# Regrouping the second expert layer of a two-layer transformer kernel: steps of 3, 4, 3 and 2 groups

## The reference

```
x: 2048 tokens of 128;  16 experts, hidden width 256, top 2
mag    = x @ bank_mag[e]
freq   = x @ bank_freq[e]
hidden = tanh(mag) * cos(softplus(freq) + 0.1 + bank_phase[e])
out    = hidden @ bank_down[e]
y      = sum over the two chosen experts of weight * out
y      = y * rsqrt(mean(y * y) + 1e-6) * norm_w
result = x + gate * y
```

## Time and profile before

| what | us |
|---|---|
| median of three runs | 714.82 (712.31 to 719.94) |
| profiled execution, whole | 713.9 |
| its span | 712.1 |
| PE busy | 493.4 |
| DVE busy | 468.7 |
| ACT busy | 336.3 |
| POOL busy | 410.8 |
| mean granted TensorE clock, share of full | 0.814 |

### The profile page before, as it was taken

How to read it: one execution, slowest core, us unless ns; L and a number is a source line. 1 busy time by engine, 2 the same in 40 slices (tenths; PEclk the granted TensorE clock), 3 DMA queues, 4 the chain that set the end, 5 groups by cost and what they waited for, 6 DMA issues and landing times.

```text
span 712.1 us, 8241 instructions
## 1 busy us (share of the span) xinstructions
PE 493.4 (69%) x2183; PEld 318.4 (45%) x2183; DVE 468.7 (66%) x911; ACT 336.3 (47%) x652; POOL 410.8 (58%) x321
## 2 busy tenths in 40 slices
PE   3577979998998899735777796269530588687410
PEld 2233323433433333524776786126530487587410
DVE  6958898898999899771332233648535566576717
ACT  3265863674675464111222235374310089589605
POOL 0039899999898989216666654612575102545650
PEclk9877989999998799856699799569555599989765
DMA  5043334442233330014656583400011555533125
GB/s 183 0 152 118 118 128 171 122 138 104 90 114 111 105 121 26 16 34 145 191 174 205 170 241 103 113 1 0 19 52 61 190 190 196 182 138 122 34 74 145
DMA packets 58384, 81.85 MB, mean 115 GB/s; under 512 B 7569, under 2 KB 32658, under 8 KB 58338
## 3 DMA queue, kind: packets, MB, share of 16 engines
q1 hardware_dynamic: 51010, 69.97, 30.2%
q0 software_dynamic: 5024, 10.30, 4.7%
q10 hardware_dynamic: 2304, 1.05, 0.5%
HBM read 57.82 MB, written 11.14 MB: 97 GB/s over the span
## 4 chain that ended last, share of the span: by engine, by line
PE 47%; DVE 15%; ACT 12%; issue 8%; another core or an unknown queue 6%; DMA 4%; POOL 4%; ACTq 2%; SPq 1%; POOLq 0%; DVEq 0%
PE ps L1128 13%; PE ps L1246 5%; PE ps L1235 4%; PE ps L1095 4%; DVE hs L1770 4%; PE ps L1404 4%; PE ps L1122 4%; PE ps L1416 2%; PE ps L1286 2%; POOL bu L568 2%; ACTq L941 1%; DVE prod L1780 1%; ACT mag L979 1%; ACT freq L981 1%
## 5 line engine op out<-in xcount | busy, mean ns | idle before, releaser
L568 POOL TENSOR_TENSOR bu<-uT,b_sb 128x1024 f32<-128x1024 f32 x64 | 150.9, 2379 | 29.0 <-DVE uT L1750 29.0
L539 POOL DMA_INDIRECT y_dram<-ys,rows_i x86 | 91.0, 1058 | 118.7 <-DVE ys L2010 70.3
L1128 PE MATMUL ps<-prod,cst 128*128 128x512 f32 x256 | 130.2, 653 | 2.9 <-DVE yT L1790 2.9
L749 ACT ACTIVATE ps<-dtT,neg_a 128x512 f32<-128x512 f32 x128 | 85.4, 684 | 50.6 <-DVE hs L1770 50.1
L1128 PEld LDWEIGHTS ps<-prod,cst 128*128 128x128 f32 x256 | 50.2, 207 | 81.5 <-issue 77.1
L579 POOL TENSOR_TENSOR prod<-hs,c_sb 128x1024 f32<-128x1024 f32 x32 | 76.6, 2394 | 15.2 <-PE ps L1128 10.8
L1770 DVE TENSOR_TENSOR_SCAN hs<-ps,carry,bu 128x512 f32<-128x512 f32 x64 | 77.6, 1262 | 4.8 <-ACT ps L749 4.5
L1770 DVE TENSOR_TENSOR_SCAN hs<-ps,bu 128x512 f32<-128x512 f32 x64 | 73.7, 1203 | 3.7 <-ACT ps L749 3.6
L1246 PE MATMUL ps<-w_s,ht 128*128 x312 | 48.5, 305 | 23.9 <-ACT ht L838 12.2
L838 ACT ACTIVATE ht<-ps,b1T 128x128 f32<-128x128 f32 x78 | 24.5, 368 | 82.4 <-PE ps L1235 45.1
L1404 PE MATMUL ps<-xt,mfr 128*128 128x128 f32 x376 | 53.1, 296 | 6.9 <-DVE freq L1973 3.2
(11 more groups left out here) (289 smaller groups left out, 856.3 us busy)
## 6 DMA issues: line engine op xcount, KB each, us to landing
b_sb<-b_rows SPq DMA_DIRECT2D x32, 512.0 KB
mfr<-mf_s SPq DMA_DIRECT2D x47, 256.0 KB
w1r<-in_w SPq DMA_DIRECT2D x39, 256.0 KB
c_sb<-b_rows SPq DMA_DIRECT2D x32, 256.0 KB
mf_s<-in_mf SPq DMA_DIRECT2D x16, 256.0 KB
xl<-x_slots SPq DMA_DIRECT2D x47, 64.0 KB
w_s<-in_w SPq DMA_DIRECT2D x9, 256.0 KB, 4.0
down_s<-in_down SPq DMA_DIRECT2D x16, 128.0 KB
```

Source lines behind the costliest of these rows:

```text
L539: pool.indirect_dma_start(y_dram[l], bass.IndirectOffsetOnAxis(ap=rows_i[:, 1, j:j + 1], axis=0), ys[:, j % slots, :], None).then_inc(save ...
L568: nc.gpsimd.tensor_tensor(bu[:, g % RING, :, :], uT[:, c % 2, :, :], b_sb[:, k % BRING, g % 2, :].unsqueeze(1).broadcast_to([P, ND, CHUNK] ...
L749: nc.scalar.activation(decay_of(g, d), dtT[:, c % 2, d, :], ACT.Exp, scale=neg_a[:, d, n:n + 1]).then_inc(S["a_ready"], 1)
L1128: last = nc.tensor.matmul(bank(Y_BANK + d), ident, prod[:, g % RING, d, :], start=n == 0, stop=n == NS - 1)
```

## The change

The steps get 3, 4, 3 and 2 groups instead of four times 3. Which groups' sines, products and down pairs a step does is given by two small functions, `trig_of` and `downs_of`. In the last step the down pairs begin one pair earlier and go two to a pair, and VectorE's third product there is made at the second pair. The last two groups, which have no step behind them, get their tanh, sine and product by pairs of tiles (`trig_pair`, `hidden_pair`) instead of by groups, and each pair's down product waits for its own pair's product alone (`hidden_done`). On VectorE the copies at the fifth and sixth pair of a step now stand ahead of the arguments there. The ring `mag` keeps its 24 tiles. The diff:

```
@@ -43,9 +43,9 @@
 GT = 4
 NG = (ST1 + GT - 1) // GT
 NPAIR = (ST1 + 1) // 2
-QG = 3
-QP = 2 * QG
-QUARTERS = NG // QG
+MAGS = 24
+STEP_GROUPS = (3, 4, 3, 2)
+LAST = 2 * (NG - STEP_GROUPS[-1])
 MR = 4
 LN_EPS = 1e-5
 RMS_EPS1 = 1e-5
@@ -278,7 +278,7 @@
         slot_i, pick_end = place("slot_i", [P, 2, NTILE], I32, at=e)
 
         mfr, e = place("mfr", [P, 2 * MR, 2 * H1], at=w_end)
-        mag, e = place("mag", [P, 2 * QG * GT, H1], at=e)
+        mag, e = place("mag", [P, MAGS, H1], at=e)
         ys1, e = place("ys1", [P, 2 * XR, C], at=e)
         inner_i, _ = place("inner_i", [P, NPACK[1]], I32, at=max(e, pick_end))
 
@@ -370,8 +370,39 @@
 
         def group_slots(g):
 
-            at = GT * g % (2 * QG * GT)
+            at = GT * g % MAGS
             return slice(at, at + group(g).stop - group(g).start)
+
+        def pair_slots(p):
+
+            at = 2 * p % MAGS
+            return slice(at, at + len(pair(p)))
+
+        def first_group(k):
+
+            return sum(STEP_GROUPS[:k])
+
+        def trig_of(k, i):
+
+            if k == 0:
+                return ()
+            first = first_group(k - 1)
+            if k == 1:
+                return (first + i,) if i < 3 else ()
+            at = ((0,), (1, 2), (3,))[i] if i < 3 else ()
+            return tuple(first + a for a in at if a < STEP_GROUPS[k - 1])
+
+        def downs_of(k, i):
+
+            if k == 0:
+                return ()
+            first, late = 2 * first_group(k - 1), 1 if k == len(STEP_GROUPS) - 1 else 2
+            at = ((0, 1), (2, 3), (4, 5) if k > 1 else (4,), (6, 7) if k > 1 else (5,))[i - late] if late <= i < late + 4 else ()
+            return tuple(first + a for a in at if a < 2 * STEP_GROUPS[k - 1])
+
+        def hidden_done(p):
+
+            return p // 2 + 1 if p < LAST else LAST // 2 + p - LAST + 1
 
         block = ctx.enter_context(nc.Block())
 
@@ -958,11 +989,11 @@
 
             def mag_copy(p):
 
-                n, at = len(pair(p)), 2 * p % (2 * QG * GT)
+                n = len(pair(p))
                 act.wait_ge(S["mag_ps1"], p + 1)
-                if p >= 2 * QP:
-                    act.wait_ge(S["dn_ps1"], p - 2 * QP + 1)
-                nc.scalar.activation(mag[:, at:at + n, :].rearrange("p a h -> p (a h)"), ps[:, 3 + p % 2 * 2, 0:n * H1],
+                if p >= MAGS // 2:
+                    act.wait_ge(S["dn_ps1"], p - MAGS // 2 + 1)
+                nc.scalar.activation(mag[:, pair_slots(p), :].rearrange("p a h -> p (a h)"), ps[:, 3 + p % 2 * 2, 0:n * H1],
                                      ACT.Copy).then_inc(S["mag_sb1"], 1)
 
             def softplus_tail(g):
@@ -980,26 +1011,35 @@
                 act.wait_ge(S["turned1"], g + 1)
                 nc.scalar.activation(freq[:, group(g), :], freq[:, group(g), :], ACT.Sin, scale=-TURN).then_inc(S["trig1"], 1)
 
+            def trig_pair(p):
+
+                js = slice(2 * p, 2 * p + len(pair(p)))
+                act.wait_ge(S["mag_sb1"], p + 1)
+                nc.scalar.activation(mag[:, pair_slots(p), :], mag[:, pair_slots(p), :], ACT.Tanh)
+                act.wait_ge(S["turned1"], p // 2 + 1)
+                nc.scalar.activation(freq[:, js, :], freq[:, js, :], ACT.Sin, scale=-TURN).then_inc(S["trig1"], 1)
+
             copy_xt1(0)
             copy_xt1(1)
-            for k in range(QUARTERS):
-                for i in range(QP):
-                    p = k * QP + i
+            for k, groups in enumerate(STEP_GROUPS):
+                g = first_group(k)
+                for i in range(2 * groups):
+                    p = 2 * g + i
                     freq_abs(p)
                     if p + 2 < NPAIR:
                         copy_xt1(p + 2)
                     mag_copy(p)
-                    if k and i < QG:
-                        trig((k - 1) * QG + i)
-                    if k and i == QG - 1:
+                    for done in trig_of(k, i):
+                        trig(done)
+                    if trig_of(k, i) and not trig_of(k, i + 1):
                         act.preload_act_table_set(LOG_EXP)
                     if i in (2, 3):
-                        softplus_tail(k * QG + i - 2)
-                    if i == QP - 1:
-                        softplus_tail(k * QG + 2)
+                        softplus_tail(g + i - 2)
+                    if i in (5, 7):
+                        softplus_tail(g + i // 2)
                 act.preload_act_table_set(SILU_TANH_SIN)
-            for g in range(NG - QG, NG):
-                trig(g)
+            for p in range(LAST, NPAIR):
+                trig_pair(p)
 
             def squares(c):
 
@@ -1407,31 +1447,28 @@
 
             def down_pair(p):
 
-                pe.wait_ge(S["hid1"], p // 2 + 1)
+                pe.wait_ge(S["hid1"], hidden_done(p))
                 if p >= 2:
                     pe.wait_ge(S["dn_sb1"], p - 1)
                 for j in pair(p):
                     e = expert1(j)
                     for k in range(FK1):
-                        last = nc.tensor.matmul(ps[:, 6 + p % 2, j % 2 * C:(j % 2 + 1) * C], mag[:, j % (2 * QG * GT), k * P:(k + 1) * P],
+                        last = nc.tensor.matmul(ps[:, 6 + p % 2, j % 2 * C:(j % 2 + 1) * C], mag[:, j % MAGS, k * P:(k + 1) * P],
                                                 down_s[:, bass.ds(e, 1), k, :].rearrange("p a c -> p (a c)"), start=k == 0, stop=k == FK1 - 1)
                 last.then_inc(S["dn_ps1"], 1)
 
             turn_pair(0)
             turn_pair(1)
             pe.wait_ge(S["in_down"], 16 * E1)
-            for k in range(QUARTERS):
-                for i in range(QP):
-                    p, d = k * QP + i, (k - 1) * QP
+            for k, groups in enumerate(STEP_GROUPS):
+                for i in range(2 * groups):
+                    p = 2 * first_group(k) + i
                     up_pair(p)
                     if p + 2 < NPAIR:
                         turn_pair(p + 2)
-                    if k and i in (2, 3):
-                        down_pair(d + 2 * i - 4)
-                        down_pair(d + 2 * i - 3)
-                    if k and i > 3:
-                        down_pair(d + i)
-            for p in range(NPAIR - QP, NPAIR):
+                    for d in downs_of(k, i):
+                        down_pair(d)
+            for p in range(LAST, NPAIR):
                 down_pair(p)
 
         @block.vector
@@ -2000,6 +2037,12 @@
                 dve.wait_ge(S["trig1"], g + 1)
                 nc.vector.tensor_tensor(m, m, freq[:, group(g), :], ALU.mult).then_inc(S["hid1"], 1)
 
+            def hidden_pair(p):
+
+                m = mag[:, pair_slots(p), :]
+                dve.wait_ge(S["trig1"], hidden_done(p))
+                nc.vector.tensor_tensor(m, m, freq[:, 2 * p:2 * p + len(pair(p)), :], ALU.mult).then_inc(S["hid1"], 1)
+
             def copy_y(p):
 
                 dve.wait_ge(S["dn_ps1"], p + 1)
@@ -2009,40 +2052,38 @@
                 n, at = len(pair(p)), 2 * p % (2 * XR)
                 nc.vector.tensor_copy(ys1[:, at:at + n, :].rearrange("p t c -> p (t c)"), ps[:, 6 + p % 2, 0:n * C]).then_inc(S["dn_sb1"], 1)
 
-            for k in range(QUARTERS):
-                for i in range(QP):
-                    p, d, g = k * QP + i, (k - 1) * QP, k * QG
-                    take_up(p)
+            for k, groups in enumerate(STEP_GROUPS):
+                g, final = first_group(k), k == len(STEP_GROUPS) - 1
+                for i in range(2 * groups):
+                    take_up(2 * g + i)
                     if i == 0 and k:
                         turns(g - 1)
+                    if k and i < 3 and i < groups:
+                        hidden(first_group(k - 1) + i)
+                    for d in downs_of(k, i):
+                        copy_y(d)
+                    if final and i == 1:
+                        hidden(first_group(k - 1) + 2)
+                    if k == 2 and i == 2:
+                        hidden(first_group(k - 1) + 3)
                     if i == 3:
-                        if k:
-                            copy_y(d + 2)
-                            copy_y(d + 3)
                         argument(g)
                         turns(g)
-                    if i == 4:
+                    if i == 4 or final and i == 3:
                         argument(g + 1)
-                        if k:
-                            copy_y(d + 4)
                     if i == 5:
                         turns(g + 1)
-                        if k:
-                            copy_y(d + 5)
                         argument(g + 2)
-                    if k and i < QG:
-                        hidden(g - QG + i)
-                    if k and i == 2:
-                        copy_y(d)
-                        copy_y(d + 1)
+                    if i == 7:
+                        turns(g + 2)
+                        argument(g + 3)
             turns(NG - 1)
-            hidden(NG - 3)
-            hidden(NG - 2)
-            copy_y(NPAIR - 6)
```

(8 more changed lines are left out.)

## The result

The changed kernel took 719.58 us in the median of 21 runs, the kernel before 714.24 in 21 runs beside it; the ratio is 1.0084 (1.0062 to 1.0107). The change made it slower by some 6 us, where 4 us of gain were forecast. The profiled execution of the changed kernel has a span of 719.9 us.

The account below looks back on a forecast made before the run. No engine is full; ScalarE paces the steady part, and the limit turns to GpSimd's scatters. Last scatter 689.66 to 685.9 is -3.8 us: 710.1 from the profiled 713.9, 711.0 from the median; forecast 710.4, range 705 to 716.

Parts of the forecast that it names:

- Step 0: First step: unchanged, nothing gained or lost; first batch of scatters still starts at about 599.50.
- the ring of 24 tiles: Buffer ring: stays 24 tiles and no product is late for it.
- step 1: Two more pairs and one more group add 4.6 us of unhidden ScalarE work.
- step 2: Four old and three new groups: 24.1 us plus 0 to 2.1 of waits, taken as 25.2.
- step 3: Two new groups behind three: 16.8 us; final load at 664.1, or 669.0 if 4.9 us of old waits return.
- 35 scatters: GpSimd's run from 634.8: 51.1 us, so the last scatter ends at 685.9 instead of 689.66.
- The hold of a scatter by a two-input VectorE instruction: GpSimd: a scatter starting inside such an instruction is held until it ends; floor 1.26 us each, second batch 1.56.
- GpSimd is never again out of work: From the second batch on: old waits of 5.88 and 4.17 us go; the wait before that batch grows by 4.6.
- ScalarE's chain ended last, and not the scatters: Rival on the kernel's end: scatters faster, 6 to 9 us gained, 704.6 to 707.7 us; chance 0.22.
- the tail: Last two groups by pairs: first copy ends 5.7 us after the final load, 7.3 in the old kernel.
- my sum with waits: Final load at 669.0 if old waits return, so the first of the last 7 tiles goes out at 675.0.
- The slow one: Rival: step 2 bound by TensorE from its third pair, up to 33.1 us, kernel 715.6 us; chance 0.10.

Follow-up runs that it names:

- chip 2: Quiet chip: the changed kernel run again beside the kernel before, 671.0 us against 671.9, ratio 0.998.
- chips 1 and 2: Two quiet chips: the changed kernel repeated against the kernel before, 671.2 us against 672.0 (0.996) and 671.0 against 671.9 (0.998).
- chip 12: Chip with the kernel before at 718.4 us: changed kernel 720.3, without second-layer scatters 697.4, with direct GpSimd transfers instead 701.1.
- after_fourth: The changed kernel run unaltered a fourth time, on chip 12, against the kernel before: 720.3 us against 718.4, ratio 1.006.

## Why the prediction was wrong

**Where it held.** Step 0 and the ring of 24 tiles went as counted, and step 1 nearly: it grew by 3.4 us in the first comparison and by 5.3 on chip 2, where I had 4.6. On chips 1 and 2 the whole schedule held: GpSimd never out of work after the second batch began, 25.4 us for step 2 (I took 25.2), 18.5 and 17.3 for step 3 (16.8), and on chip 2 35 scatters in 48.4 us (51.1 forecast, a mean of 1.39 each with the gap instead of 1.47). Yet the gain there is 0.2 and 0.4% by the ratios, because the old steps lacked their waits on these chips too. The hold of a scatter by a two-input VectorE instruction is seen again: the one of 646.18 ended at 647.85, 0.83 after VectorE's of 645.79 with 1.23.

**The step that failed** is step 2's "between 0 and 2.1 us of waits". It came to 30.7 us, 6.6 beyond its work of 24.1, and to 28.2 on chip 12. I had seen that step 1 waited 9 us and step 3 4.9 beyond its work, named the places and carried them over as if they belonged to the places: step 1's waits were kept, step 3's too in the later of my two values, and step 2's were taken from the old step 2. They go with the trains of scatters. In the old schedule two of the three trains beside running steps showed them, 11.2 us over the steps of chip 2 (81.7 against 70.4). In the new one all three did: 87.7 against 72.3, 15.4 us, and 85.1 on chip 12, 12.8. Without the indexed scatters they are gone on chip 12; the chip of the first comparison was not tried so. From that follows the rest. "GpSimd is never again out of work" failed on these chips alone, with idle times of 1.98, 4.62, 1.96 and 2.21; ScalarE's chain ended last, and not the scatters: the first copy of the tail was done at 687.65, against 669.0 + 5.7 = 674.7 in my sum with waits, 679.3 when the 4.6 us later start of this execution is added. Of the 8.3 us between, 3.3 are the tail's, below, and 5.0 the steps'.

**A term mis-sized on every chip** is the tail. From the final load to the end of the first copy I had 5.7 us; it took 9.0 on chip 2 (626.38 to 635.41) and 9.0 in the first comparison (678.65 to 687.65). The rows of the first comparison, then the copy on chip 2:

```profile
678.62 1.22 DVE L2022 SCALAR_TENSOR_TENSOR freq<-fabs,freq 128x1024 f32<-128x1024 f32 x1
...
684.19 1.29 DVE L2044 TENSOR_TENSOR mag<-mag,freq 128x512 f32<-128x512 f32 x2
685.12 5.51 PE L1456 MATMUL ps<-down_s,mag 128*128 x28 [6.88 <-DVE mag L2044]
687.23 0.42 DVE L2053 COPY ys<-ps 128x256 f32<-128x256 f32 x1 [1.74 <-PE ps L1456]
```

```profile
634.99 0.42 DVE L2053 COPY ys<-ps 128x256 f32<-128x256 f32 x1 [1.75 <-PE ps L1456]
```

Most of it, 2.1 us, lies ahead of the first product, which began 5.5 us after the load and not 3.4: the arguments and turns of both groups start only when the load does, because the copies of pairs 18 and 19 stand ahead of them. And TensorE comes back from 6.88 us of idleness slowly: from its first matmul at 685.12 to VectorE's copy are 2.1 us, not 1.1, in a stretch (684 to 690) of a granted clock of 0.59, near the lower of its two levels. On quiet chips GpSimd's train hid this almost exactly; on the others nothing does. The old tail took 7.3.

**The rivals.** The slow one had the place right (step 2 too long, decided from 31.4 us) and the mechanism wrong: by its rows TensorE had time to spare (21.5 us busy of 30.7 in step 2), and what it signalled came late. Step 2 came to 30.7, and step 3 and the tail added the rest.

**What stays open.** The stretch of scatters is 2.5 us longer in the first pair of traces, and 1.2 us shorter in after_fourth than in the one trace of before on such a chip; the measured ratios say 4.6 to 6. So the late signals in the steps are shown, but that they make up the whole loss is not. The traces are single executions with 8.7 us of spread ahead of the stage, so how the loss divides is argued from step lengths, not summed. Both kernels without scatters on such a chip would have settled it. Why the old second train showed no late signal was not found. Nor is it known what in those chips delays the signal.

## What to carry to other kernels

A wait that the records don't explain must be tied to what ran beside it before its place is moved: ask which neighbour it comes with, not which step it stood in. A schedule that packs GpSimd's scatters tightly is good where they are the bound and bad where they disturb; time it on more than one chip, for here a loss of 0.6 to 0.8% on two chips was nothing, or a gain of up to 0.4%, on two others. Count a tail from the last instruction that its engine has ahead of it, not from the load that opens it.

## What the runs showed of the hardware

Two kinds of chips ran the same program in 672 us and in 714 to 718. Up to about 312 us of the span, where no indexed transfer is made yet, the two traces of the kernel before agree to 3 us; the rest opens behind it, in the stretches with indexed transfers. The longest late signal is in unchanged code, in the second layer's routing. ScalarE's waits of the kernel before in the first comparison, of all the program (engine, line, what it waited for: us in total, times, longest):

```profile
ACT h_tok L900 <- remote: 20.1, 1, 20.1
```

It ends at 541.80, 3.2 us after the end of a long train of scatters (the last one from 537.60, 0.96 long); TensorE's product that it waits for is recorded as done at 531.7. On chip 2 the longest wait of the same line was 6.7 us. From these two waits I estimate that some 10 us could be gained there on such chips with a looser train; that was not tried.
